# Sparse experts with routing counts read ahead of the norm, list transfers issued earlier, and attention's row of maxima sent by ScalarE

## The chip, the cores and the metric

The kernel runs on one core of one Trainium2 chip. The metric is the device time of one execution in microseconds (us). The engines are TensorE (PE, its weight loads PEld), VectorE (DVE), ScalarE (ACT), GpSimd (POOL) and SyncE (SP, which here only issues DMAs). Each engine works through its own list in order; semaphores tie them together.

## The reference

Six blocks on x of shape (16, 512, 256), each with a residual and a layer norm ahead of it: FFN, gated linear attention (GLA), FFN, experts, softmax attention, experts. The change touches the last three. Cut to what matters:

```python
def experts(x):                       # run twice: ahead of attention and behind it
    logits = x @ router_w + router_b                  # 8 experts, 8192 tokens
    topk_vals, topk_idx = top_k(logits, 2)
    gates = softmax(only the two chosen logits)
    routed = sum over the 2 chosen e: gates[e] * (silu(x @ w1[e]) * (x @ w3[e])) @ w2[e]
    shared = sum over 2 shared s:     (silu(x @ w1[s]) * (x @ w3[s])) @ w2[s]
    return routed + shared

def attention(x):                     # 16 sequences, 16 heads of 16
    scores = q @ k.T / 4 + band       # band: 0.1 where |i - j| <= 2
    return softmax(scores) @ v @ Wo.T + bo
```

All is float32; the kernel splits each matmul operand in a high and a low part (three matmuls for one product).

## The kernel before, in words

**Stages.** The blocks run one after another, with a barrier between them. x stays in SBUF. A batch is 512 tokens (4 tiles of 128); there are 16.

**Expert stage (`moe_stage`), first half, per batch b.** TensorE's list is: `hidden(b, 0)`, which is 12 matmuls of 512 columns for shared expert 0 (6 into h1, 6 into h3) with the 16 small router matmuls woven in; `output(b-1, 0)`; `transposes(b+1)`; `hidden(b, 1)`; `output(b-1, 1)`; `counts(b)`, which counts the tokens that each expert got. VectorE's list is: `product(b-1, 1)`; `normalise(b+1)` (L1152); `rows(b-1)` (L1190 to L1197), which reads the counts, adds them to `run` and works out the row of each token in its expert's list; `add_shared(b-2, 1)` (L1210); `product(b, 0)` (L1204); `choose(b)` (L1164 to L1185), which ranks the logits; `add_shared(b-1, 0)`; `low(b+1)` (L1159). ScalarE does silu (L1012), the high part of the activations (`act_high`, L1018), the high part of the transposed norm (L1007) and the two gates (L1023, L1024), with a table load at each change between silu and sigmoid. GpSimd does the low parts of the activations (`act_low`, L1108, one for each shared expert) and issues, for each batch, eight indirect DMAs (`enlist`, L1116) that write the normed rows to the experts' lists in HBM. Its order is `act_low(b, 0)`, `enlist(b-1)`, `act_low(b, 1)`.

Three waits order this: `hidden(b, 0)` starts with a wait for `counts_read` of batch b-1, which L1192 sets (the router writes the PSUM bank of the counts); `normalise(b)` waits until the lists of batch b-3 are written, since the buffer `m_rows` has three turns; and `output(b, 0)` waits for both low parts.

**Expert stage, second half.** When all counts are known, VectorE works out tables (L1243 to L1266), then 68 pairs of slots are loaded from the lists, put through their expert and scattered to `results`; then each token's two results are loaded and added.

**Attention (`att_stage`), per sequence.** 16 steps (4 groups of heads x 4 tiles) of two turns each. In each turn TensorE issues a pair of `s2` score matmuls for step st (L1642, which ScalarE turns to exponentials, L1804) and a pair of `s1` matmuls for step st+7 (L1628, from which VectorE takes the negated row maximum, L1898). The maxima of a group are transposed (L1653), copied by ScalarE (`max_copy`, L1814) and sent by a DMA into the row of `q_stack` that makes s2 come out with the maximum taken off (`max_row`, L1479, two DMAs from SP). Between them lie the transposes of the group's output (`out_t`, L1678, which also waits for `max_copy` of the group two further on) and the projections of the next sequence. q and k of the next sequence are written to HBM by SP (L1458) and read back in stacked form (L1471). SP's list for a sequence:

```python
def body(b, before, more):
    max_row(b, 1)
    write(b + 1, 0, x, False) for both x
    max_row(b, 2)
    write(b + 1, 0, x, True) for both x
    load(b + 1, 0); load(b + 1, 1)
    max_row(b, 3)
    ...
```

Of the kernel before, what the change touches and what calls it, by code (L numbers as in the profile page):

```python
# [77 lines left out]
def as_f32(ap):  # L78
    return ap.bitcast(F32)
# [579 lines left out]
ID_COL, ROW_COL = DM, DM + 1  # L659


def moe_stage(core, a, name, out=None):

# [8 lines left out]
    ROOM = ALL_TILES * P + P  # L672
    N_SLOTS = TOP_K * ALL_TILES + EXPERTS
    PAIRS = N_SLOTS // 2
# [3 lines left out]
    with ExitStack() as ctx:  # L678
# [11 lines left out]

        lists = nc.dram_tensor(name + "_lists", (EXPERTS * (ROOM + P), PITCH), F32).ap()
        results = nc.dram_tensor(name + "_results", (DUMMY + 2 * EXPERTS * TOP_K * P, DM), F32).ap()
# [22 lines left out]
        run_i = core.sbuf("run_i", [P, EXPERTS], I32, ctx)  # L715
        zeros = core.sbuf("zeros", [P, DM], F32, ctx)
        pad = core.sbuf("pad", [P, 2 * EXPERTS, PITCH - DM], F32, ctx)
        steps_of = core.sbuf("steps_of", [P, ALL_TILES], F32, ctx)
# [3 lines left out]
        over = core.sbuf("over", [P, EXPERTS, ALL_TILES], BF16, ctx)  # L722
# [7 lines left out]
        slot_lane_row = core.sbuf("slot_lane_row", [P, N_SLOTS], F32, ctx)  # L730
        slot_e_i = core.sbuf("slot_e_i", [P, N_SLOTS], I32, ctx)
        slot_row_i = core.sbuf("slot_row_i", [P, N_SLOTS], I32, ctx)
# [33 lines left out]
        high_ready, low_ready, y_ready, y_free = (s(f"{name}_{n}") for n in ("high", "low", "y", "y_free"))  # L766
# [25 lines left out]

        def results_of_pair(i):
            return results_written[i % YS_RING], 32 * (i // YS_RING + 1)

        with nc.Block() as block:

            @block.sync
            def _(sp):
# [4 lines left out]
                for e in range(EXPERTS):  # L804
                    rest = slice(EXPERTS * ROOM + e * P, EXPERTS * ROOM + (e + 1) * P)
                    sp.dma_start(lists[rest, 0:DM], zeros[:, :]).then_inc(padded, 16)
                    sp.dma_start(lists[rest, DM:PITCH], pad[:, EXPERTS + e, :]).then_inc(padded, 16)
                sp.wait_ge(run_ready, 1)
                for e in range(EXPERTS):
                    first = sp.value_load(run_i[0:1, e:e + 1], min_val=0, max_val=EXPERTS * ROOM - P)  # L810
                    sp.dma_start(lists[bass.ds(first, P), 0:DM], zeros[:, :]).then_inc(padded, 16)
                    sp.dma_start(lists[bass.ds(first, P), DM:PITCH], pad[:, e, :]).then_inc(padded, 16)
                sp.wait_ge(slots_ready, 1)
                sp.wait_ge(padded, 16 * 4 * EXPERTS)
                for r in range(XS_RING):
                    sp.wait_ge(listed[r], 16 * TILES * TOP_K * len(range(r, B, XS_RING)))
                for i in range(PAIRS):
                    if i >= XT_RING:
                        sp.wait_ge(t2_ready, i - XT_RING + 1)
                        sp.wait_ge(ids_ready, i - XT_RING + 1)  # L820
                    for j in range(2):
                        n = 2 * i + j
                        first = sp.value_load(slot_row_i[0:1, n:n + 1], min_val=0, max_val=EXPERTS * (ROOM + P) - P)
# [3 lines left out]
                by_lane = results[0:DUMMY, :].rearrange("(p n c) d -> p n c d", p=P, c=TOP_K)  # L827
                for i in range(PAIRS - YS_RING, PAIRS):
                    sp.wait_ge(*results_of_pair(i))
                if out is not None:  # L830
                    rows = out.rearrange("(n p) d -> p n d", p=P)
                for u in range(UNITS):
# [5 lines left out]
                    if out is not None and u >= YB_RING and (u - YB_RING) % 2 == 1:  # L838
                        tiles = slice((u - YB_RING - 1) * 2, (u - YB_RING + 1) * 2)
                        sp.dma_start(rows[:, tiles, :], core.x[:, tiles, :]).then_inc(stored, 16)  # L840
                if out is not None:
# [6 lines left out]
            def _(pe):  # L848
# [23 lines left out]
                def hidden(b, e):  # L872
# [3 lines left out]
                    if b:  # L876
                        pe.wait_ge(act_ready, 2 * (b - 1) + e + 1)
                        if e == 0:
                            pe.wait_ge(counts_read, b)
                    n = 0  # L880
                    for i, acc in enumerate((h1, h3)):
                        for k in range(KT):
                            for m, (w, x) in enumerate([(w13h, xh[p]), (w13l, xh[p]), (w13h, xl[p])]):
# [4 lines left out]
                                if e == 0:  # L888
                                    for _ in range(1 if n < 8 else 2):
# [89 lines left out]
                pe.wait_ge(slots_ready, 1)  # L979
# [20 lines left out]
            def _(act):  # L1000
# [42 lines left out]
                act.wait_ge(low_ready, 2 * B)  # L1043
# [24 lines left out]
            def _(pool):  # L1068
# [25 lines left out]
                link(g.iota(steps_of[:, :], pattern=[[P, ALL_TILES]], base=0, channel_multiplier=0,  # L1094
# [7 lines left out]
                link(g.iota(pad[:, :, 0], pattern=[[TOP_K * P, 2 * EXPERTS]], base=DUMMY, channel_multiplier=TOP_K,  # L1102
                            allow_small_or_imprecise_dtypes=True))

                def act_low(b, e):
                    pool.wait_ge(high_ready, 2 * b + e + 1)
                    slot = 2 * (b % 2) + e
                    nc.gpsimd.tensor_tensor(al[:, slot, :], act_f[:, e, :], as_f32(ah[:, slot, :]),  # L1108
                                            ALU.subtract).then_inc(low_ready, 1)
# [1542 lines left out]
```

## Time and profile before

| | |
|---|---|
| time before, median of 3 runs | 4055.28 us (4054.49 to 4057.51) |
| the profiled execution's own time | 4069.08 us |
| its span, first to last instruction | 4067.3 us |
| mean granted TensorE clock | 0.863 of full |
| busy shares of the span | PE 76%, DVE 61%, ACT 42%, POOL 38% |

Times inside the profile are counted from the span's start. Idle time stands just before the instruction that ended it, with what released it behind the arrow.

### The profile page before, as it was taken

To read this page: it belongs to the slowest core of one execution; us is meant where nothing else is said; L and a number is where in the kernel's file an instruction comes from. 1 tells how busy PE (TensorE), PEld (TensorE's weight loads), DVE (VectorE), ACT (ScalarE), POOL (GpSimd) and SP (SyncE) were. 2 spreads that over 40 slices of the span, in tenths; PEclk is the share of its full clock that TensorE was granted. 3 is DMA by queue.
4 is the path that set the end of the run, shared out by engine and by line. 5 is a ranking of instruction groups with operands and counts; after the bars stand their busy time and mean duration, and the time that the engine had idled before them with its cause. 6 is when DMAs were issued, how large, how long until landed. Compare 5 with 4: busy or idle time off the path is not lost. (4 is left out here: it accounts for less than half of the span.)

```text
span 4067.3 us, 73679 instructions
## 1 busy us (share of the span) xinstructions
PE 3094.8 (76%) x24796; PEld 2326.5 (57%) x24796; DVE 2478.4 (61%) x5047; ACT 1704.1 (42%) x2711; POOL 1564.5 (38%) x1380
## 2 busy tenths in 40 slices
PE   6998788886999566679417888888888875667892
PEld 4887677775888455579412333343333334556791
DVE  5665677776676444455656767666666644444566
ACT  2444344443455222246204555555555543222461
POOL 2555222221566344456312333333333322444561
PEclk9999899998999666689757999999999986666896
DMA  3000000000000111146533233332332302111568
GB/s 105 0 0 10 6 0 0 0 0 1 1 0 0 60 42 42 42 129 189 183 116 84 77 94 79 91 88 74 89 93 69 94 25 71 42 43 43 160 192 285
DMA packets 163468, 276.45 MB, mean 68 GB/s; under 512 B 28752, under 2 KB 100832, under 8 KB 163312
## 3 DMA queue, kind: packets, MB, share of 16 engines
q1 hardware_dynamic: 137968, 204.71, 18.2%
q0 software_dynamic: 25344, 69.76, 5.0%
q8 instruction: 85, 1.39, 0.2%
q14 instruction: 71, 0.58, 0.0%
HBM read 141.15 MB, written 132.71 MB: 67 GB/s over the span
## 5 line engine op out<-in xcount | busy, mean ns | idle before, releaser
L1898 DVE TENSOR_REDUCE neg_max_sb<-s_ps 128x2 f32<-128x1024 f32 x512 | 627.6, 1226 | 383.3 <-PE s_ps L1628 377.8
L1804 ACT ACTIVATE prob_sb<-s_ps 128x1024 f32<-128x1024 f32 x512 | 524.8, 1025 | 507.5 <-PE s_ps L1642 502.2
L1539 POOL TENSOR_TENSOR prob_sb<-prob_sb,band_sb 128x520 f32<-128x520 f32 (+1 forms) x256 | 284.9, 1113 | 728.6 <-ACT prob_sb L1804 728.6
L533 POOL TENSOR_TENSOR f_sq_lo_sb<-f_sq_sb,f_sq_hi_sb 128x512 fp32r<-128x512 f32 x256 | 329.2, 1294 | 349.7 <-ACT f_sq_hi_sb L508 349.6
L884 PE MATMUL moe_h_ps<-xnT_hi_sb,w13h_sb 128*128 128x512 f32 x256 | 150.9, 590 | 238.4 <-DVE run_sb L1192 234.4
L1628 PE MATMUL s_ps<-k_stack_sb,q_stack_sb 48*128 48x512 f32 x1024 | 249.0, 482 | 107.4 <-DMA k_stack_sb<-qk_scratch 53.6
L1130 POOL DMA_INDIRECT moe_results<-m_rows_sb,result_id_sb x272 | 260.8, 959 | 154.4 <-DVE result_id_sb L1281 100.5
L1665 PE MATMUL pv_ps<-prob_sb,v_ones_sb 128*32 128x512 f32 x2048 | 292.9, 646 | 1.4 <-POOL prob_sb L1539 1.3
L1642 PE MATMUL s_ps<-q_stack_sb,k_stack_sb 64*128 64x512 f32 x1024 | 267.0, 518 | 33.4 <-ACT prob_sb L1804 33.0
L1642 PEld LDWEIGHTS s_ps<-q_stack_sb,k_stack_sb 64*128 64x128 f32 x1024 | 99.4, 191 | 328.0 <-ACT prob_sb L1804 201.6
L503 ACT ACTIVATE f_relu_sb<-ffn_hp_ps 128x512 f32<-128x512 f32 x256 | 153.4, 599 | 314.7 <-PE ffn_hp_ps L456 314.1
L1116 POOL DMA_INDIRECT moe_lists<-m_rows_sb,row_i_sb x256 | 248.6, 971 | 73.3 <-issue 73.3
L570 DVE TENSOR_TENSOR f_sq_sb<-ffn_hp_ps,f_relu_sb 128x512 f32<-128x512 f32 x256 | 174.8, 687 | 134.3 <-ACT f_relu_sb L503 99.5
L468 PE MATMUL ffn_y_ps<-w_proj_tern_sb,f_sq_lo_sb 128*128 128x256 f32 x1024 | 256.1, 283 | 0.0
L468 PE MATMUL ffn_y_ps<-w_proj_tern_sb,f_sq_hi_sb 128*128 128x256 f32 x1024 | 255.1, 282 | 0.7 <-POOL f_sq_lo_sb L533 0.7
L1108 POOL TENSOR_TENSOR m_act_lo_sb<-m_act_sb,m_act_hi_sb 128x512 fp32r<-128x512 f32 x64 | 90.1, 1408 | 400.9 <-ACT m_act_hi_sb L1018 400.2
L456 PE MATMUL ffn_hp_ps<-xnT_hi_sb,w_fc_hi_sb 128*128 128x512 f32 x512 | 210.7, 412 | 20.6 <-DVE xnT_lo_sb L162 19.8
L1012 ACT ACTIVATE m_silu_sb<-moe_h_ps 128x512 f32<-128x512 f32 x64 | 38.2, 597 | 447.7 <-PE moe_h_ps L884 447.4
L1204 DVE TENSOR_TENSOR m_act_sb<-moe_h_ps,m_silu_sb 128x512 f32<-128x512 f32 x64 | 44.3, 692 | 282.0 <-ACT m_silu_sb L1012 264.7
L884 PEld LDWEIGHTS moe_h_ps<-xnT_hi_sb,w13h_sb 128*128 128x128 f32 x256 | 65.1, 254 | 251.4 <-issue 236.3
L1628 PEld LDWEIGHTS s_ps<-k_stack_sb,q_stack_sb 48*128 48x128 f32 x1024 | 104.1, 200 | 182.6 <-DVE neg_max_sb L1898 120.1
L456 PE MATMUL ffn_hp_ps<-xnT_hi_sb,w_fc_lo_sb 128*128 128x512 f32 x512 | 203.9, 398 | 0.0
(353 smaller groups left out, 8964.7 us busy)
## 6 DMA issues: line engine op xcount, KB each, us to landing
m_rows_sb<-moe_lists SPq DMA_DIRECT2D x272, 130.0 KB
qk_scratch<-qk_hi_sb SPq DMA_DIRECT2D x128, 256.0 KB
q_stack_sb<-qk_scratch SPq DMA_DIRECT2D x128, 192.0 KB, 3.6
k_stack_sb<-qk_scratch SPq DMA_DIRECT2D x128, 192.0 KB, 4.6
xnT_hi_sb<-moe_results SPq DMA_DIRECT2D x32, 512.0 KB, 3.8
xnT_lo_sb<-moe_results SPq DMA_DIRECT2D x32, 512.0 KB, 5.1
qk_scratch<-qk_lo_sb SPq DMA_DIRECT2D x64, 256.0 KB
x_resident_sb<-x SPq DMA_DIRECT2D x4, 2048.0 KB, 17.8
```

The lines of the kernel that those rows point to most:

```text
L456: op = nc.tensor.matmul(hp[j % 2][:, :], a[:, k, j * P:(j + 1) * P], x[:, k, :], start=(k == 0 and i == 0), stop=(k == KT - 1 and i == 2))
L468: op = nc.tensor.matmul(y[:, t, :], r[:, j, t * P:(t + 1) * P], w.proj[:, j, :], start=(j == 0 and t % 2 == 0 and i == 0), stop=(j == JT - ...
L533: nc.gpsimd.tensor_tensor(sql[:, j, :], sq[:, j % 2, :], as_f32(sqh[:, j, :]), ALU.subtract).then_inc(low_ready, 1)
L884: op = nc.tensor.matmul(acc[e][:, :], w[:, EXPERTS + e, k, i, :], x[:, k, :], start=(k == 0 and m == 0), stop=(k == KT - 1 and m == 2))
L1116: g.indirect_dma_start(lists, bass.IndirectOffsetOnAxis(row_i[:, r, t, c:c + 1], 0), xs[:, r, t, :], None).then_inc(listed[r], 16)
L1130: g.indirect_dma_start(results, bass.IndirectOffsetOnAxis(result_id[:, i % ID_RING, j:j + 1], 0), rows_out[:, i % YS_RING, j, :], None).th ...
L1539: nc.gpsimd.tensor_tensor(pr, pr, bcast(band[:, off:off + hi - lo].unsqueeze(1), [P, GH, hi - lo]), ALU.mult).then_inc(band_done, 1)
L1628: op = nc.tensor.matmul(s1p[:, half, :], qs[r, g // 2, at, qt * P:(qt + 1) * P], ks[r, g // 2, at, :], start=True, stop=True)
L1642: op = nc.tensor.matmul(s2p[:, half, :], ks[r, g // 2, at, kt * P:(kt + 1) * P], qs[r, g // 2, at, :], start=True, stop=True)
L1665: op = nc.tensor.matmul(pvp[2 * HD * i:2 * HD * (i + 1), :], vaug[:, kt, GH * g + i, :], prob[:, kt, i, :], start=(kt == 0), stop=(kt == T ...
L1804: nc.scalar.activation(prob[:, kt, pair(t), :], s2p[:, :, :], ACT.Exp).then_inc(exp_done, 1)
L1898: nc.vector.tensor_reduce(nm[:, g % 2, pair(t), qt], s1p[:, :, :], AXIS_X, ALU.max, negate=True).then_inc(max_done, 1)
```

## The change

What it does, with one "wave" (`WAVES = 1`), so that the new loops over waves run once:

- VectorE: `rows(b-1)` stands ahead of `normalise(b+1)`; behind it a new `act_low(b-1)` makes the low part of shared expert 1.
- GpSimd: one low part for each batch (expert 0), and `enlist(b-1)` ahead of it. The semaphore of the low parts is split in two.
- TensorE: `hidden(b, 0)` waits for the counts to be read behind the 7th matmul, not ahead of the 1st, and all 16 router matmuls stand among the last 6.
- Tables: one small copy more (`run` is reset), and two casts become adds.
- Second half: the order of waits on SP is a little different; the work is the same.
- Attention: `max_copy` moves up one turn; `max_row` goes from SP to ScalarE, two turns' places: behind the exponentials of (st % 4 == 2, first turn).

```diff
# TensorE, hidden(b, e)
                     if b:
                         pe.wait_ge(act_ready, 2 * (b - 1) + e + 1)
-                        if e == 0:
-                            pe.wait_ge(counts_read, b)
...
-                                if e == 0:
-                                    for _ in range(1 if n < 8 else 2):
+                                if e == 0 and i == 1:
+                                    if b and n == 0:
+                                        pe.wait_ge(counts_read, b)
+                                    for _ in range(2 if n < 4 else 3):
                                         router(b, n)
# TensorE, output(b, half)
-                        pe.wait_ge(low_ready, 2 * b + 2)
+                        for e in range(SHARED):
+                            pe.wait_ge(low_ready[e], b + 1)
# GpSimd
                 for b in range(B):
-                    act_low(b, 0)
                     if b:
                         enlist(b - 1)
-                    act_low(b, 1)
+                    act_low(b)
                 enlist(B - 1)
# VectorE
+                def act_low(b):
+                    dve.wait_ge(high_ready, 2 * b + 2)
+                    slot = 2 * (b % 2) + 1
+                    v.tensor_tensor(al[:, slot, :], act_f[:, 1, :], as_f32(ah[:, slot, :]),
+                                    ALU.subtract).then_inc(low_ready[1], 1)
...
                     if b:
                         product(b - 1, 1)
+                        rows(b - 1)
+                        act_low(b - 1)
                     if b + 1 < B:
                         normalise(b + 1)
-                    if b:
-                        rows(b - 1)
                     if b >= 2:
                         add_shared(b - 2, 1)
                     product(b, 0)
# tables
+                    link2(v.tensor_copy(run[:, :], first_row[:, :]))
# attention, SP
                 def body(b, before, more):
-                    max_row(b, 1)
...
+                    for m in range(KT):
+                        if more:
+                            for low in (False, True):
+                                for x in range(2):
+                                    write(b + 1, m, x, low)
+                            load(b + 1, 2 * m)
+                            load(b + 1, 2 * m + 1)
# attention, ScalarE
+                def max_row(b, g):
+                    act.wait_ge(nmt_ready, b * GROUPS + g + 1)
+                    hold(act, row_turns)
+                    places = slice(place(g, 0), place(g, 0) + 2)
+                    for half in range(2):
+                        row, of = 64 * half + STACK, slice(half * 2 * TILES, (half + 1) * 2 * TILES)
+                        act.dma_start(as_f32(qs[row:row + 1, g // 2, places, :]),
+                                      as_f32(nmt[of, g % 2, :])).then_inc(rowed[g], 16)
...
-                            if st % TILES == 2 and t == 0:
-                                if st - 1 + TILES < STEPS:
-                                    max_copy(b, st // TILES + 1)
+                            if st % TILES == 1 and t == 1 or st % TILES == 2 and t == 0:
+                                step = max_copy if t else max_row
+                                if st // TILES + 1 < GROUPS:
+                                    step(b, st // TILES + 1)
                                 elif more:
-                                    max_copy(b + 1, 0)
+                                    step(b + 1, 0)
```

## Rows read from the trace of the kernel before

**Rows 1.** Windows by stage: busy us (count) of PE, PEld, DVE, ACT, POOL; clock, DMA.
```profile
1365.00:1760.00 395.00, 265.55 (x1208) 234.53 (x1208) 167.59 (x496) 103.26 (x161) 160.23 (x165) 0.67 0.12 43
2160.00:3300.00 1140.00, 963.14 (x5530) 437.89 (x5532) 773.95 (x931) 625.57 (x779) 382.38 (x320) 0.93 0.33 83
3375.00:3770.00 395.00, 264.41 (x1208) 232.77 (x1208) 167.06 (x495) 103.26 (x161) 159.55 (x163) 0.68 0.12 43
```

**Rows 2.** The waits of 1395 to 1757: us in total, times, longest.
```profile
PE moe_h_ps L884 <- DVE run_sb L1192: 110.4, 14, 8.8
DVE m_rows_sb L1152 <- DMA moe_lists<-m_rows_sb,row_i_sb: 73.1, 13, 6.3
```

**Rows 3.** The timeline of one batch, VectorE and GpSimd: start, duration.
```profile
1581.48 0.69 DVE L1204 TENSOR_TENSOR m_act_sb<-moe_h_ps,m_silu_sb 128x512 f32<-128x512 f32 x1 [7.93 <-ACT m_silu_sb L1012]
1582.09 0.18 DVE L1164 TENSOR_TENSOR logits_sb<-moe_misc_ps,router_b_sb 128x32 f32<-128x32 f32 x1
...
1586.60 0.75 DVE L1210 SCALAR_TENSOR_TENSOR x_resident_sb<-moe_y_ps,x_resident_sb 128x256 f32<-128x256 f32 x2
...
1595.92 1.38 DVE L1152 TENSOR_SCALAR m_rows_sb<-x_resident_sb,ln_mean_var_sb,ln_rstd_sb 128x256 f32<-128x256 f32 x4 [6.06 <-DMA moe_lists<-m_rows_sb,row_i_sb]
...
1582.90 1.52 POOL L1108 TENSOR_TENSOR m_act_lo_sb<-m_act_sb,m_act_hi_sb 128x512 fp32r<-128x512 f32 x1 [12.68 <-ACT m_act_hi_sb L1018]
...
1593.46 0.96 POOL L1116 DMA_INDIRECT moe_lists<-m_rows_sb,row_i_sb  x1 [0.30 <-issue]
```

**Rows 4.** Windows inside two batches, columns as in rows 1.
```profile
1572.30:1583.10 10.80, 10.73 (x38) 9.60 (x39) 2.73 (x11) 1.22 (x2) 0.20 (x1) 0.50 0.00 0
1583.10:1589.00 5.90, 5.77 (x38) 4.86 (x37) 5.20 (x13) 4.41 (x7) 4.83 (x5) 0.98 0.19 67
1589.00:1597.50 8.50, 0.22 (x6) 0.12 (x5) 2.24 (x7) 0.75 (x2) 5.47 (x6) 0.77 0.22 79
```

**Rows 5.** The timeline of the stage's last batch, which has no `normalise`.
```profile
1743.22 0.17 DVE L1192 TENSOR_TENSOR run_sb<-moe_misc_ps,run_sb 128x8 f32<-128x8 f32 x1
1743.54 0.47 PE L884 MATMUL moe_h_ps<-xnT_hi_sb,w13h_sb 128*128 128x512 f32 x1 [1.43 <-DVE run_sb L1192]
1748.12 0.60 ACT L1012 ACTIVATE m_silu_sb<-moe_h_ps 128x512 f32<-128x512 f32 x1 [4.38 <-PE moe_h_ps L884]
1757.08 0.17 DVE L1192 TENSOR_TENSOR run_sb<-moe_misc_ps,run_sb 128x8 f32<-128x8 f32 x1
1763.48 1.85 POOL L1116 DMA_INDIRECT moe_lists<-m_rows_sb,row_i_sb  x1 [0.16 <-issue]
```

**Rows 6.** Two lines: duration ns min/median/max, first and last start.
```profile
L1192 DVE TENSOR_TENSOR run_sb<-moe_misc_ps,run_sb x32: 166/166/168, 1393.4 to 3767.7; 128x8 f32<-128x8 f32 x32
L1479 SPq DMA_DIRECT2D q_stack_sb<-neg_max_t_sb x128: 634/674/1061, 2146.3 to 3314.5; - x128
```

**Rows 7.** Windows in GLA and in attention, columns as in rows 1.
```profile
455.00:970.00 515.00, 424.61 (x8600) 370.90 (x8598) 402.42 (x845) 214.51 (x351) 121.39 (x101) 1.00 0.00 0
2863.70:2870.00 6.30, 6.25 (x21) 2.90 (x21) 2.45 (x2) 1.60 (x2) 0.73 (x1) 0.50 0.30 64
```

**Rows 8.** The waits of 2202 to 3240, attention's inner sequences.
```profile
PE misc_ps L1678 <- ACT neg_max_t_sb L1814: 58.4, 56, 1.1
PE s_ps L1628 <- DMA k_stack_sb<-qk_scratch: 40.2, 14, 3.3
```

**Rows 9.** One of the page's costliest groups: busy us, mean ns, idle before.
```profile
L1804 ACT ACTIVATE prob_sb<-s_ps 128x1024 f32<-128x1024 f32 x512 | 524.8, 1025 | 507.5 <-PE s_ps L1642 502.2
```

**Rows 10.** The timeline of SP's issues between two sequences.
```profile
2850.14 1.76 SPq L1479 DMA_DIRECT2D q_stack_sb<-neg_max_t_sb  x2
2852.04 1.33 SPq L1458 DMA_DIRECT2D qk_scratch<-qk_lo_sb  x2
```

**Rows 11.** The timeline of ScalarE in the batch of rows 3.
```profile
1585.63 1.28 ACT L1023 ACT_TABLE_LOAD   x1
1586.92 0.21 ACT L1023 ACTIVATE gates_sb<-lead_sb 128x4 f32<-128x4 f32 x1
```

More of the change, by code:

```diff
@@ L765, in moe_stage @@
         h_ready, silu_ready, act_ready = (s(f"{name}_{n}") for n in ("h", "silu", "act"))
-        high_ready, low_ready, y_ready, y_free = (s(f"{name}_{n}") for n in ("high", "low", "y", "y_free"))
+        high_ready, y_ready, y_free = (s(f"{name}_{n}") for n in ("high", "y", "y_free"))
+        low_ready = [s(f"{name}_low{e}") for e in range(SHARED)]
         logits_ready, chosen_ready, counts_ready, counts_read = (
@@ L803, in _, with load_rows @@
                 sp.wait_ge(consts, CONSTS)
[L804 to L814, printed above, removed]
+                for w in range(WAVES):
+                    for e in range(EXPERTS):
+                        row = w * WAVE_ROWS + EXPERTS * ROOM + e * P
+                        sp.dma_start(lists[row:row + P, 0:DM], zeros[:, :]).then_inc(padded, 16)
+                        sp.dma_start(lists[row:row + P, DM:PITCH],
+                                     pad[:, (2 * w + 1) * EXPERTS + e, :]).then_inc(padded, 16)
+                for w in range(WAVES):
+                    sp.wait_ge(run_ready, w + 1)
+                    for e in range(EXPERTS):
+                        first = sp.value_load(run_i[0:1, w, e:e + 1], min_val=0, max_val=WAVES * WAVE_ROWS - P)
+                        sp.dma_start(lists[bass.ds(first, P), 0:DM], zeros[:, :]).then_inc(padded, 16)
+                        sp.dma_start(lists[bass.ds(first, P), DM:PITCH],
+                                     pad[:, 2 * w * EXPERTS + e, :]).then_inc(padded, 16)
+                sp.wait_ge(padded, 16 * 4 * EXPERTS * WAVES)
                 for r in range(XS_RING):
                     sp.wait_ge(listed[r], 16 * TILES * TOP_K * len(range(r, B, XS_RING)))
-                for i in range(PAIRS):
+                by_lane = results[0:DUMMY, :].rearrange("(p n c) d -> p n c d", p=P, c=TOP_K)
+                if out is not None:
+                    rows = out.rearrange("(n p) d -> p n d", p=P)
+                def load_rows(i):
                     if i >= XT_RING:
@@ L822, in _, with load_results @@
                         n = 2 * i + j
-                        first = sp.value_load(slot_row_i[0:1, n:n + 1], min_val=0, max_val=EXPERTS * (ROOM + P) - P)
+                        first = sp.value_load(slot_row_i[0:1, n:n + 1], min_val=0, max_val=WAVES * WAVE_ROWS - P)
                         sp.dma_start(rows_in[:, i % XT_RING, j, :], lists[bass.ds(first, P), :]).then_inc(
                             rows_in_loaded[i % XT_RING], 16)
[L827 to L832, printed above, removed]
+                def load_results(u):
+                    w = u // WAVE_UNITS
+                    if u % WAVE_UNITS == 0:
+                        for i in range((w + 1) * WAVE_PAIRS - YS_RING, (w + 1) * WAVE_PAIRS):
+                            sp.wait_ge(*results_of_pair(i))
                     if u >= YB_RING:
@@ L837, in _ @@
                         results_loaded[u % YB_RING], 16)
-                    if out is not None and u >= YB_RING and (u - YB_RING) % 2 == 1:
+                    if out is not None and u >= YB_RING and u % 2:
                         tiles = slice((u - YB_RING - 1) * 2, (u - YB_RING + 1) * 2)
                         sp.dma_start(rows[:, tiles, :], core.x[:, tiles, :]).then_inc(stored, 16)
+                sp.wait_ge(slots_ready, WAVES)
+                for i in range(PAIRS):
+                    load_rows(i)
+                    if unit_at(i + 1) is not None:
+                        load_results(unit_at(i + 1))
+                for u in range(UNITS - WAVE_UNITS, UNITS):
+                    load_results(u)
                 if out is not None:
@@ L1472, in load @@
                                          scratch[m, x, :, :, heads, :]).then_inc(loaded[g], 16)
-                def max_row(b, g):
-                    sp.wait_ge(nmt_ready, b * GROUPS + g + 1)
-                    places = slice(place(g, 0), place(g, 0) + 2)
-                    for half in range(2):
-                        row, of = 64 * half + STACK, slice(half * 2 * TILES, (half + 1) * 2 * TILES)
-                        sp.dma_start(as_f32(qs[row:row + 1, g // 2, places, :]),
-                                     as_f32(nmt[of, g % 2, :])).then_inc(rowed[g], 16)
                 for m in range(KT):
```

180 lines of the change are left out of this document (93 added, 87 removed).

## The prediction, made before the changed kernel was run

> **What bounds the kernel now.** I read the page first (no engine is busy throughout), then the windows by stage, then the waits inside the stages that the diff touches, then one batch in order of time.
>
> The windows show where time is lost [rows 1]: each expert stage's first half takes about 395 us with TensorE busy 265 of them, and that at a granted clock of 0.67, so much of the busy time is slow matmuls. Attention has 963 busy of 1140 us at 0.93. The waits name the loss [rows 2]: in one first half TensorE stands 110 us before `hidden(b, 0)` until L1192 has read the counts, and VectorE stands 73 us before `normalise` until the lists of three batches back are written. One batch in order of time shows that these are one chain [rows 3]. `act_low(b, 0)` starts at 1582.90, only then come the eight list DMAs, 0.30 and 0.96 us each, the last at 1593.46; it lands about 1.5 us after its 0.96, `normalise` runs at 1595.92, `rows` behind it, and only then `hidden(b+1, 0)`. So a batch lasts as long as hidden + silu + product + low part + eight DMAs + landing + norm. The clock makes it worse [rows 4]: after the idle 8.5 us the next 10.8 us run at 0.50, until TensorE has been busy a while.
>
> The interval is (1743.2 - 1393.4)/14 = 25.0 us for 14 batches [rows 5, 6]. The last batch has no `normalise` and so no list wait ahead of `rows`; it took 1757.08 - 1743.22 = 13.9 us [rows 5]. This is the nearest thing in the trace to the changed order.
>
> **The change in the first half.** With `rows` first and `enlist(b-1)` ahead of `act_low(b)`, list DMAs start as soon as the rows are known, a whole interval before `normalise` asks for them. I add up what each engine must do for a batch at full clock:
>
> - VectorE: product 0.61, choose 4.51 (1582.09 to 1586.60), add 0.7, low 1.3 (two of the product's size), product 0.6, rows 1.0 (six small ones like L1192's 0.17), norm 1.4, add 0.7 come to 10.8, and the new `act_low`, two operands of 128x512 like the product, is 0.69: 11.5 [rows 3, 5].
> - GpSimd: 8 x 1.26 + one low part of 1.5 = 11.7 (before: 13.2) [rows 3].
> - TensorE: half of 10.7 slow plus 5.8 fast is 11.1 [rows 4]. Of it `hidden(b, 0)` is 4.58 from first matmul to silu [rows 5]; the rest I share out by columns as an estimate: `hidden(b, 1)` 2.7, two outputs at 1.4, transposes 1.0, counts 0.4. With latencies 11.4.
>
> All three lie close together, so the interval is a loop through them. The longest that I find starts at silu(b, 0): silu and product 0.63 + 0.61, choose 4.51, `add_shared` 0.75 (which frees y), `output(b-1, 1)` 1.4, counts 0.4, `hidden(b+1, 0)` 4.58 to its silu. That is 12.9, with five crossings of some 0.05 us 13.2. The counts no longer lie on it: L1192 is done about 9.3 us after silu(b, 0), and the 7th matmul ends about 10. The list wait does not either: eight DMAs from the rows on take 10.3, landing 1.5, so 11.8 us against an interval of 13.2 plus the 0.7 of `act_low`. The spare is only 2 us. TensorE then has one gap of about 1.9 us per batch (y not yet free).
>
> The clock decides the rest. Between two levels: at full clock 13.2. If the lower one held all the time TensorE would be busy throughout at 22.8. The evidence is divided. In GLA 515 us passed at 1.00 with TensorE busy 82% [rows 7], and here it would be 11.4/13.2 = 86%. In attention, behind a stall of 2.9 us, 6.3 us ran at 0.50 [rows 7]. The gap here is 1.9 us, shorter than that stall but once in each batch. TensorE's part of the loop is 6.4 us, so a mean clock of 0.9 gives 13.9. I take 14.0.
>
> Per stage: 363.7 us from the first L1192 to the last before [rows 5, 6], 15 x 14.0 = 210 after: 154 saved. The last batch's lists start at 1763.5 before, because two low parts and the batch before's lists stand in front [rows 5]; after, they start with the rows at about 1758: 5 more. The stage enters at the lower clock and stays there a batch or so: 5 back. The extra copy in the tables is 0.2. So 154 a stage, **308** for two; the second stage's windows repeat the first's [rows 1]. In the second half nothing is on another engine than before: 0.
>
> **Attention.** Two waits of TensorE change [rows 8]. `out_t` waits for `max_copy`, 58.4 us in 56 places, 1.04 each: the copy stood behind an exponential of 1.03 us [rows 9]. It moves ahead of it, so the wait goes. At three of the four places of a sequence the step has work to fill in; at the step with the other stall, it is swallowed. Second, `s1` waits for the stacked k, 2.9 us in each of 14 sequences. On SP the low writes stood behind `max_row`: 2850.14 against 2852.04 [rows 10]. Taking the row away brings writes, loads and landing forward by 1.9 us. Together 3 x 0.9 + 1.9 = 4.6 us per sequence; a part will turn into other waits, since the step's two turns also hang on VectorE's maxima, so I take 3.8, x 15 = **57**.
>
> What ScalarE pays: two issues per group. SP needs 0.67 us for one [rows 6]; no row shows a DMA issued by ScalarE. If its sequencer issues while the exponential runs (1.03 us), 1.35 us is hidden in that and in the gap of over 1 us before the next one; if it waits for it, each group loses 1.35 on the exp loop, 5.4 a sequence, which takes all the 4.6 and a little more. Above: 4.6 and, without the slow 6.3 us behind the stall [rows 7], up to 3 more. So attention gains from -15 to 115, and I take 57, nearer to hidden. The Trainium skill says ("DMA: Bandwidth & Descriptors", section "Issuing engines are not separate DMA queues") that spreading issues over engines saves only the issuing sequencer's time. By that rule alone, attention would gain at most SP's 1.76 us per sequence [rows 10], 26 us, and not 57; the rule leaves out that the order of SP's list, and `max_copy`'s place on ScalarE, change too.
>
> One more rule speaks against my interval. ScalarE loads two tables per batch, which delays silu(b, 1). The row says 1.28 and the next ACTIVATE 0.01 us behind it [rows 11]. The skill ("ScalarE: Activation LUTs", section "What ACT_TABLE_LOAD costs") adds a drain of about 1.38 us to each switch; estimated by that page, silu(b, 1), the product and the rows would come 2.8 us later and the interval would be about 15.7. The trace does not have this drain, and it decides; what a late silu would do is inside rival 1's interval.
>
> **Sum.** 308 + 57 = 365. Against the profiled execution's own 4069.1 that is 3704; the median of the runs lies 13.8 lower, so **3690** there (-9.0%).
>
> **The rivals.**
>
> 1. *The clock doesn't hold.* The gap of 1.9 us and the stretch of small router matmuls just ahead of it bring the lower level in every batch. For it: before, ten slow us passed with TensorE 99% busy in just such work before the clock rose [rows 4]. Against: GLA. With a mean of 0.7 TensorE's 6.4 us are 9.1 and the interval about 16.3: 119 a stage with the ends left at 0, total 4055 - 238 - 40 = 3777. The skill ("TensorE: Matmul & The Clock Gate", section "HAM oscillation — how this bites in real kernels") also tells of kernels that fall back in each turn of a loop; in rows 4 this one does. Held at 0.5 throughout, 22.8: 3975.
> 2. *ScalarE's issues stand in the exp loop*, above: attention gains nothing or loses 15, total 4055 - 308 + 8 = 3755.
> 3. *GpSimd or the lists become the bound.* The lists of one batch are written twice as often. A list DMA took 1.85 us in one place, beside a bf16 table instruction of VectorE [rows 5]. At 1.85 each the interval is 8 x 1.85 + 1.5 = 16.3: like rival 1, 3775. **Slower than before** it gets only when GpSimd's `enlist` needs over 3.1 us for each DMA: the mean interval before, 363.7/15 = 24.2, and 57/30 = 1.9 for attention's gain make 26.1, less 1.5 for the low part, over 8. At 3.5 us the interval is 29.5 and the total 4055 + 30 x 5.3 - 57 = 4157. Nothing in the rows goes that far.
> 4. *The change does nothing*: the wait for the lists only moves, since `normalise` still stands on VectorE ahead of `product(b, 0)`. It would need landing some 10 us later than now. 4055 within 0.2%.
>
> **Chances.** My forecast (interval 13.2 to 14.8, attention 20 to 110; 3625 to 3735) 0.58; rival 1 0.17, of which the lower level throughout 0.03; rival 2 0.14; rival 3 0.06, of which slower 0.02; rival 4 0.02; the remaining 0.03 is for more than I foresee (clock at 1.00 in attention too). Range: 3620 to 3800 takes in the forecast, rival 2 and most of rivals 1 and 3. Under 0.2% (8 us) a measurement of this kernel can't tell from no change. Faster 0.96, same 0.015, slower 0.025.
>
> **What would show it.** The interval of L1192 (or its line after) from 25.0 to 13 to 15 us; the clock of the first halves from 0.67 to 0.9 or more; no wait of TensorE for `run` over 1 us, and one of about 1.9 before `output(b-1, 1)` for the residual add; VectorE's wait before `normalise` under 1 us; each first half at 235 to 250 us. In attention: no wait of `out_t` for the row of maxima, the wait for the stacked k at 1 to 1.5 us, exponentials no later behind ScalarE's issues. The prediction is wrong if the clock falls in each batch, if the list DMAs stretch, or if L1804 is held up at every fourth step.

## The result, and the profile after

The changed kernel takes 3667.5 us (median of 4 runs, 3658.1 to 3674.2) against 4056.4 us for the kernel before on the same chip: a ratio of 0.904, interval 0.902 to 0.906. The forecast was 3690 in a range of 3620 to 3800. The profiled execution is the fastest of the four, 3658.1 us with a span of 3656.3 and so 9.4 below the median, where that of before was 12.7 above its own (4069.1 against 4056.4). So 22 of the 411 us between the two spans lie in which executions were profiled, and 389 in the kernels.

The windows of the changed kernel by stage (us of the window, busy us and count of PE, PEld, DVE, ACT and POOL, granted clock, DMA share, GB/s). They stand against [rows 1]:

```profile
1390.00:1584.00 194.00, 181.26 (x1147) 161.67 (x1145) 155.16 (x481) 95.79 (x150) 139.15 (x136) 0.94 0.23 83
1960.00:3070.00 1110.00, 971.56 (x5510) 444.35 (x5510) 780.26 (x937) 623.20 (x775) 379.76 (x318) 0.92 0.34 87
3165.00:3365.00 200.00, 183.94 (x1177) 163.47 (x1176) 163.78 (x502) 100.27 (x157) 142.66 (x138) 0.95 0.23 82
```

In the first half TensorE is now busy 93% of the time, not 67%, and its clock is 0.94, not 0.67. The busy time fell too. From the first count of the stage to the last, so over the same matmuls, it went from 250 to 180 us: most of them are no longer run at half speed. Here is the line that reads the counts, L1224 (L1192 before), against the first row of [rows 6]:

```profile
L1224 DVE TENSOR_TENSOR run_sb<-moe_misc_ps,run_sb x32: 166/166/169, 1391.4 to 3359.8; 128x8 f32<-128x8 f32 x32
```

Within a stage it comes 15 intervals apart from 1391.4 to 1581.2 and from 3173.2 to 3359.8: 12.65 and 12.44 us on average, where the first 14 were 25.0.

The batches are not alike. Here are three of these intervals in a row (columns as above):

```profile
1481.50:1493.10 11.60, 11.38 (x78) 10.01 (x77) 9.98 (x33) 6.36 (x11) 8.27 (x9) 1.00 0.23 81
1493.10:1505.40 12.30, 11.58 (x79) 10.40 (x78) 10.57 (x33) 6.37 (x11) 9.24 (x10) 1.00 0.24 88
1505.40:1519.10 13.70, 12.80 (x79) 11.66 (x78) 10.59 (x33) 6.42 (x11) 10.19 (x10) 0.88 0.25 90
```

In the third the clock was 0.50 for 3.4 us. Over both stages, 11 of the 30 intervals hold a stretch at 0.50 and last 13.7 us on average; the other 19 hold none and last 11.9. So the mean clock of 0.94 is 1.00 with such stretches in it.

The waits in the first stage's batches, 1391 to 1583 us, against [rows 2]:

```profile
DVE m_act_sb L1237 <- ACT m_silu_sb L1044: 31.4, 23, 2.7
...
PE moe_y_ps L944 <- DVE x_resident_sb L1249: 9.2, 15, 1.1
...
DVE m_rows_sb L1184 <- DMA moe_lists<-m_rows_sb,row_i_sb: 0.9, 1, 0.9
...
PE moe_misc_ps L898 <- DVE run_sb L1224: 0.2, 1, 0.2
```

The 110 us of TensorE for the counts and the 73 us of VectorE for the lists are gone. What is left to TensorE is a wait for the residual add, at most 1.1 us in each batch.

By place, the span lost 2.0 us ahead of the first L1224 (L1192), 173.9 in the first stage's batches, 54.3 from there to the second stage's first batch, 177.6 in the second stage's batches and 3.1 behind them. Of the 54.3, attention's 15 sequences hold 41.3 (from the first second-pass matmul to that of the last sequence, 1112.2 us before and 1070.9 after). The waits of attention's inner sequences, 2050 to 2990 us, show that the one for the row of maxima, 58 us in [rows 8], has no row any more. The one for the stacked k, 3.2 us in each of 13 sequences, has not shrunk (2.9 before):

```profile
PE s_ps L1659 <- DMA k_stack_sb<-qk_scratch: 41.7, 13, 3.7
PE s_ps L1673 <- ACT prob_sb L1835: 31.4, 53, 0.9
PE s_ps L1659 <- DVE neg_max_sb L1940: 24.5, 29, 1.3
```

### The profile page after: what moved, and what is told of

Read it like the earlier page. It is cut to its first block and busy times, and to the rows that moved or that the text cites. A ratio compares the mean times of both kernels' runs of the same rounds, so it can differ in the third digit from the quotient of the medians.

```text
span 3656.3 us, 73695 instructions
## 1 busy us (share of the span) xinstructions
PE 2955.9 (81%) x24796; PEld 2208.2 (60%) x24796; DVE 2474.6 (68%) x5081; ACT 1704.4 (47%) x2711; POOL 1521.9 (42%) x1348
## 5 line engine op out<-in xcount | busy, mean ns | idle before, releaser
L456 PE MATMUL ffn_hp_ps<-xnT_lo_sb,w_fc_hi_sb 128*128 128x512 f32 x512 | 201.6, 394 | 0.0
L468 PEld LDWEIGHTS ffn_y_ps<-w_proj_tern_sb,f_sq_hi_sb 128*128 128x128 f32 x1024 | 194.4, 190 | 11.9 <-POOL f_sq_lo_sb L533 1.1
L468 PEld LDWEIGHTS ffn_y_ps<-w_proj_tern_sb,f_sq_lo_sb 128*128 128x128 f32 x1024 | 195.2, 191 | 10.0
L2458 POOL TENSOR_TENSOR g_ks_sb<-g_ks_sb,g_tot_sb 128x512 f32<-128x512 f32 x96 | 109.1, 1137 | 178.0 <-PE g_h_ps L2206 117.6
L200 DVE BATCH_NORM_STATS2 ln_stat_sb<-x_resident_sb 128x6 f32 (+1 forms) x384 | 138.2, 412 | 35.6 <-POOL x_resident_sb L541 21.7
```

The source lines that it names most:

```text
L456: op = nc.tensor.matmul(hp[j % 2][:, :], a[:, k, j * P:(j + 1) * P], x[:, k, :], start=(k == 0 and i == 0), stop=(k == KT - 1 and i == 2))
L468: op = nc.tensor.matmul(y[:, t, :], r[:, j, t * P:(t + 1) * P], w.proj[:, j, :], start=(j == 0 and t % 2 == 0 and i == 0), stop=(j == JT - ...
```

## The experiments

**The two parts alone.** `m_only` takes all expert edits and leaves attention as before, `a_only` the reverse.

> The expert stages changed, attention as before. If the two parts do not touch each other (theory A), the interval between batches in the first halves is 12.6 us as in the changed kernel's trace, each first half 174 to 178 us shorter, and attention's sequences last 75 us as before: about 3712 us. My prediction's sizes (308 us for the experts) would give 3748 us. If attention's change had also helped the experts (clock, queues), it would be above 3760.

> Attention changed, the expert stages as before. Theory A: sequences of 71.6 us as in the changed kernel's trace, 41 us less, about 4015 us. My prediction's size (57 us) would give 3999 us. TensorE's wait for the stacked k stays near 3 us in each sequence if the writes' transfer bounds it, and falls to 1 to 1.5 us if SP's order does.

`m_only` took 3702.7 us (ratio 0.9125, interval 0.9105 to 0.9144) and `a_only` 4022.1 (0.9915, 0.9892 to 0.9938), with 4061.4 for the kernel before in these runs. So the experts give 359 us and attention 39, both near theory A. They add up to 398, against 389 measured with both; each of the three has an interval of 8 us or more to either side, so the 9 us between them are not clear of noise. The intervals between batches in `m_only` are those of the full change (12.4 on average), and no run shows the two parts touching each other.

**The two halves of attention's edit.** `copy_early` is the kernel before with `max_copy` one turn earlier, and SP still sends the row. `row_act` leaves the copy at its old place, and ScalarE sends the row behind it. The edit of `copy_early`:

```diff
-                            if st % TILES == 2 and t == 0:
+                            if st % TILES == 1 and t == 1:
                                 if st - 1 + TILES < STEPS:
                                     max_copy(b, st // TILES + 1)
```

> The kernel before with one edit: ScalarE copies the row of maxima one turn earlier; SP still sends it, in the old order. Theory B (the copy's place is the whole of attention's gain): as a_only, some 41 us, 4015 us. Rival (my prediction: 2.7 us of a sequence from the copy, 1.9 from SP's freed order): about 33 us less than before, 4023 us, and a_only 15 to 25 us below it.

> The kernel before with the other edit alone: ScalarE sends the row, behind the copy at its old place, and SP's list is free of it. Theory B: SP's low writes start some 2 us earlier, but land no earlier, the wait for the stacked k stays at 2.9 us, and the time stays within 5 us of before (4051 to 4061 us). Rival (my prediction): 1.9 us of each sequence, 28 us less, 4028 us. If ScalarE's issues stand in the way of the exponentials: slower by up to 5.4 us a sequence, 4135 us.

`copy_early` took 4025.0 us (0.9912, 0.9881 to 0.9943), the gain of `a_only` but for 3 us. In the two profiled executions the 15 sequences are 7 us longer in `copy_early` (1078.4 against 1071.4), so the row's move may have a small part of its own beside the copy; neither number is clear of noise. `row_act` took 4074.7 (1.0033, 1.0021 to 1.0046), 13 us slower than before, where theory B had said no change. Its waits of 2202 to 3240 us, against [rows 8]:

```profile
PE misc_ps L1658 <- ACT neg_max_t_sb L1794: 58.3, 56, 1.1
...
PE s_ps L1608 <- DMA k_stack_sb<-qk_scratch: 23.1, 13, 2.4
...
PEld s_ps L1622 <- DMA q_stack_sb<-neg_max_t_sb: 18.4, 13, 1.7
```

The wait for the row of maxima stays. The one for the stacked k falls by some 17 us and comes back as a wait for the row itself, which ScalarE now sends late. Timed from the end of the keys' cast (`high_part` of x = 1), which is what makes the writes possible, the mean over 14 sequences is:

| from the end of the cast, us | before | row_act | after |
|---|---|---|---|
| first low write issued | 3.55 | 1.42 | 1.42 |
| first load issued | 9.18 | 9.09 | 8.90 |
| group 0 of the stack landed | 15.15 | 15.10 | 14.87 |

SP's list without the row issues the low writes 2.1 us earlier, and the loads start when they did. What they wait for is not SP.

**The order on GpSimd.** `low_first` is the changed kernel with `act_low(b)` ahead of `enlist(b-1)` again.

```diff
 for b in range(B):
+    act_low(b)
     if b:
         enlist(b - 1)
-    act_low(b)
```

> The changed kernel with GpSimd's low part of batch b put back ahead of the list DMAs of batch b-1. Theory C (this order closed the chain of before): list DMAs of b-1 start only behind hidden, silu, product, cast and low part of b, the norm two batches on waits for their landing, and the next low part hangs on that: 10.3 + 1.5 + norm 1.4 + add 0.7 + product 0.65 + cast 1.35 + low part 1.4 = some 17.5 us, more at a lower clock: 17.5 to 19 us for a batch, 150 to 190 us more than the changed kernel, 3815 to 3860 us. Rival D (VectorE's order, rows ahead of the norm, did it): within 30 us of the changed kernel, 3670 to 3700 us.

It took 3771.0 us (0.9287, 0.9267 to 0.9307): 104 of the 389 us gained are lost, more than D said and less than C. The mean interval of the first stage is 16.1. The waits of its batches, 1394 to 1629 us:

```profile
POOL m_act_lo_sb L1141 <- ACT m_act_hi_sb L1050: 77.2, 15, 10.5
...
PE moe_y_ps L944 <- DVE x_resident_sb L1249: 45.9, 15, 4.7
...
DVE m_rows_sb L1184 <- DMA moe_lists<-m_rows_sb,row_i_sb: 41.7, 13, 4.9
```

GpSimd stands in front of its low part with the lists ready behind it, and the wait for the lists is back. Two more things are in the 3.6 us that a batch got longer: one multiply of `choose` costs 1.0 more (last section), and 28 of the 30 intervals hold a stretch at the clock of 0.50, where 11 did. That it stops at 16 and not at 25 fits `rows` no longer waiting behind `normalise`; no run has both orders put back.

**The order on VectorE.** `norm_first` is the changed kernel with `rows(b-1)` and the new `act_low` behind `normalise(b+1)`.

```diff
         product(b - 1, 1)
-        rows(b - 1)
-        act_low(b - 1)
     if b + 1 < B:
         normalise(b + 1)
+    if b:
+        rows(b - 1)
+        act_low(b - 1)
```

> The changed kernel with VectorE's rows put back behind the norm. Theory C: the lists start 1.4 us later and so the loop lists 10.3 + landing 1.5 + norm 1.4 = 13.3 us decides: 0.6 us more for a batch, 20 us more in all, 3690 us. Rival D: counts are read late again, most of the gain of the experts is gone, over 3850 us.

3732.8 us (0.919, 0.917 to 0.921), interval 14.6 and 14.8 in the two stages: 65 us lost, where C said 20 and D over 180. Waits of 1394 to 1612 us:

```profile
PE moe_misc_ps L898 <- DVE run_sb L1224: 21.6, 14, 2.5
DVE m_rows_sb L1184 <- DMA moe_lists<-m_rows_sb,row_i_sb: 9.4, 8, 1.9
```

The wait of TensorE for the counts, which is D's, is back at 1.5 us in each of 14 batches; C's wait for the lists comes in 8 and is shorter. Each batch lasts 2.1 us longer, and 19 of the 30 intervals hold a stretch at 0.50. So the result lies between the two theories, nearer to C by its size and to D by its waits. With the lists started early, `normalise` ahead of `rows` costs 65 us; with `rows` ahead, a late start of the lists costs 104. Either order, kept with the other edits, holds most of the gain.

**The place of the wait on TensorE.** `wait_head` makes the counts wait ahead of all of `hidden(b, 0)`, as before, and spreads the router's matmuls over it.

```diff
         pe.wait_ge(act_ready, 2 * (b - 1) + e + 1)
+        if e == 0:
+            pe.wait_ge(counts_read, b)
```

> The changed kernel with TensorE's wait for the counts back at the head of the first hidden matmuls and the router spread over all of them. By my prediction's walk the counts are read 9.3 us behind the silu and the matmuls could start at 8.4: 0.9 us of each batch where it lies on the loop: 15 to 27 us more, 3685 to 3695 us. Rival: TensorE has other waits to fill, nothing to see (within 8 us of 3667).

3685.7 us (0.9073, 0.9056 to 0.909), 18 us for it, as expected (14 by the ratios). But the trace puts the cost elsewhere: the first intervals of the two stages are 17.6 and 16.6 us, at the low clock, against 11.2 and 12.3, and make 11 us. Behind them TensorE waits 0.9 us for the counts in each batch, the clock stays at 1.00, and every interval is 12.9, against 12.6 on average in the changed kernel with its stretches at 0.50.

**The low part on VectorE.** `pool_both` puts the second low part back on GpSimd.

```diff
 def act_low(b):
-    pool.wait_ge(high_ready, 2 * b + 1)
+    for e in range(SHARED):
+        pool.wait_ge(high_ready, 2 * b + e + 1)
```

> The changed kernel with both low parts on GpSimd. GpSimd then needs 8 x 1.26 + 2 x 1.35 and its own waits, 13.3 us for a batch, and the low parts lie beside more of VectorE's two-operand work. Theory E (GpSimd becomes the bound, and VectorE's operations with both operands in SBUF stretch beside its subtraction as the multiply of choose did before, 1.38 against 0.42): 13.3 to 14.3 us, 20 to 50 us more, 3690 to 3720 us, and the stretched operations show in the trace. Rival F (VectorE was the long pole with 11.5 us and is relieved of 0.69): 10 to 20 us less, 3650 us.

3695.1 us (0.9093, 0.9067 to 0.9119), 28 us more, and steady intervals of 13.7 in the second stage (13.5 on average in the first, from 11.2 to 16.2): theory E. GpSimd then waits only some 0.9 us of such an interval, for the cast; eight DMAs with their issues and two low parts fill the rest. Each of these intervals also holds 3.4 us at the clock of 0.50, and how much of the 13.7 is that was not separated.

**The sigmoids off the path.** `gates_late` is the changed kernel with one pair of sigmoids at the end of the first half, over all batches, in the place of a pair in each batch. Its result stands in the table below, with those of the next two.

```diff
-                    share(b)
                     silu_of(b, 1)
                     act_high(b, 1)
+                share()
```

> The changed kernel, with the two sigmoids of each batch put off to the end of the first half (one pair of sigmoids over all batches; nothing is left out). In the changed kernel two table loads of 1.28 us each and the sigmoids stand on ScalarE ahead of the second silu of each batch, and VectorE waits 31 us a stage for silu. Theory G, what is left between batches is partly this wait: the interval falls from 12.5 to 11.8 or 12.0, where TensorE's own 11.7 us of work per batch stops it; 2 stages x 15 x 0.6 = 18 us, so 3640 to 3655 us. Rival H, TensorE's work alone sets the interval and VectorE's wait is idle time that costs nothing: 3663 to 3672 us, interval 12.4 to 12.7.

**The keys' cast one exponential earlier.** `high_early` is the changed kernel with this edit of ScalarE's order in attention; `late_and_early` has both edits.

```diff
+                            if more and at in ((4, 0), (5, 0)):
+                                high_part(b + 1, 0, st - 4)
                             if st % TILES == 1 and t == 0:
                                 if st > 1:
                                     ot_copy(b, st // TILES - 1)
...
-                            if more and at in ((4, 0), (5, 1)):
-                                high_part(b + 1, 0, t)
```

> The changed kernel, with the cast of the keys' high part for the next sequence made one exponential earlier (behind the first exponential of the sixth step, ahead of the copy of the output; nothing is left out). The stacked keys are waited for 3.1 us in each sequence. Theory T, the chain of transfers from that cast to the loaded stack (14.9 us, whatever SP's order) sets the wait: the cast ends 2.0 us earlier, the stacked keys land 1.5 to 2.0 us earlier, the wait falls to 1.1 to 1.6 us, and 15 x 1.5 to 2.0 makes 22 to 30 us: 3637 to 3645 us. Rival S, the transfers are set by something other than that cast (the queue's other loads, the rows of maxima): wait 2.8 to 3.1 us and 3663 to 3672 us. Rival X, the cast ahead of the output's copy delays the exponentials by 0.6 us a sequence or more: above 3672 us or the gain less than half.

> Both edits of the two runs beside this one in one kernel. If both theories hold they add: 3667 less 18 less 26 is 3623 us, range 3610 to 3640. If either fails, the other's time alone.

| kernel | median us | ratio to before | interval |
|---|---|---|---|
| changed kernel | 3667.5 | 0.9039 | 0.9017 to 0.906 |
| gates_late | 3649.6 | 0.8993 | 0.897 to 0.9016 |
| high_early | 3612.8 | 0.891 | 0.8883 to 0.8937 |
| late_and_early | 3605.2 | 0.8885 | 0.8864 to 0.8907 |

`gates_late`: the mean intervals fell from 12.65 and 12.44 to 12.37 and 12.24, 7 us in all. The spans differ by 5 and the medians by 18. It is nearer to H by the traces: the intervals without a stretch at 0.50 went from 11.88 to 11.78 on average, 0.1 us and not 0.6, and the long ones, 13.0 to 16.1, are those with such a stretch, 7 where 11 had one. It is a small gain whose size these runs don't settle.

`high_early` gave 55 us (45 by the spans of the profiled executions), about twice what theory T said. T was right in its place. The stack lands 14.98 us behind the cast, as in the changed kernel (14.87), the cast ends 1.9 us earlier, and TensorE's wait fell from 3.1 to 1.2 us per sequence. But the mean sequence got 3.0 us shorter, 71.4 to 68.4, and only 1.9 of that is the wait. The windows show the rest. First the changed kernel, ending its wait at 2665.6 (columns as above):

```profile
2662.60:2665.00 2.40, 0.00 (x0) 0.00 (x0) 0.22 (x1) 1.27 (x2) 0.31 (x1) 1.00 1.03 201
2665.60:2667.60 2.00, 2.00 (x7) 1.43 (x8) 1.23 (x1) 0.00 (x0) 0.00 (x0) 0.72 1.07 203
2667.60:2669.60 2.00, 2.00 (x7) 0.76 (x5) 0.00 (x0) 0.26 (x1) 0.00 (x0) 0.50 0.18 37
2669.60:2671.60 2.00, 2.00 (x15) 0.55 (x13) 1.23 (x1) 1.57 (x4) 1.11 (x1) 0.92 0.00 0
```

And the same steps of the same sequence in `high_early`, its wait ending at 2633.9:

```profile
2630.90:2633.30 2.40, 1.62 (x12) 0.34 (x10) 1.88 (x2) 1.75 (x2) 1.12 (x1) 1.00 1.00 215
2633.90:2635.90 2.00, 1.97 (x8) 1.24 (x8) 1.23 (x1) 0.17 (x1) 0.00 (x0) 1.00 1.01 209
2635.90:2637.90 2.00, 2.00 (x16) 0.65 (x15) 1.20 (x1) 1.44 (x3) 0.34 (x1) 1.00 0.03 6
2637.90:2639.90 2.00, 2.00 (x16) 1.57 (x18) 1.26 (x2) 1.35 (x3) 0.79 (x1) 1.00 0.01 2
```

Behind the wait of 3.3 us TensorE's clock falls to 0.50 (1.2 GHz) for 3.4 us, and in a window of 2 us at that clock seven matmuls pass where sixteen do at 2.4 GHz. Over the 15 sequences the two add up: the waits for the stack fell from 46.3 to 17.6 us, 28.7 less, and the time at 0.50 from 152.5 to 121.1 us, which at half speed is 15.7 us of TensorE's work. Together they make 44.4, and the sequences got 44.6 us shorter.

But a long wait doesn't always bring the low clock, nor a short one spare it. In the changed kernel such a stretch lies at 14 of the 15 waits (1.7 to 3.7 us), not at one of 2.84. In `row_act` it lies at the 11 waits of 1.59 to 2.43 us and at none of the four of 0.15 to 1.09. In `high_early` it lies at two of 14, 1.51 and 1.83, and not at 1.62 or 2.05. `late_and_early` has the best time of all, 3605.2 us, though no more than 8 us below `high_early`; it lies 5 us under the range expected, since `high_early` alone gave more than was put in.

## Why the prediction was right, and where its numbers were off

**The loop through the list DMAs was the bound: right.** Both waits went, the clock of the first halves rose to 0.94 and 0.95, and `low_first` and `norm_first` bring the waits back one at a time. So rival 4 fell too. Each wait comes back in part, and no run puts back both orders. The first halves' batches gave 351.5 us by the spans, where the prediction took 308 with their ends. Of these ends it took 5 us saved at the tail and 5 given back at the entry. Neither came. The lists of the first stage end 4.2 us sooner behind the last count, but the first load from them starts 19.6 us behind it, where it was 19.4; and the first batches of a stage (11.2 and 12.3 us) are no longer than the mean. The 13.0 us that the spans show between the stages beside attention's 15 sequences (54.3 - 41.3) lie in its last sequence (4.5) and between attention and the next stage's first count (8.2). `m_only`, with attention as before, has 4.5 and 7.2 in the same places; what makes them is open.

**The interval, forecast 14.0, is 12.55.** One batch checks the forecast's loop term by term. It ran at the clock of 1.00, for which the forecast said 13.2, and TensorE waits in it for the residual add (0.72 us), so the loop has no slack there. The changed kernel's ScalarE, VectorE and GpSimd in order of time:

```profile
1496.57 0.60 ACT L1044 ACTIVATE m_silu_sb<-moe_h_ps 128x512 f32<-128x512 f32 x1 [2.86 <-PE moe_h_ps L913]
...
1508.67 0.60 ACT L1044 ACTIVATE m_silu_sb<-moe_h_ps 128x512 f32<-128x512 f32 x1 [2.66 <-PE moe_h_ps L913]
...
1497.85 0.17 DVE L1196 TENSOR_TENSOR logits_sb<-moe_misc_ps,router_b_sb 128x32 f32<-128x32 f32 x1
...
1499.08 0.43 DVE L1203 TENSOR_TENSOR notless_sb<-notless_sb,earlier_sb 128x256 f32<-128x256 f32 x1
...
1501.40 0.75 DVE L1249 SCALAR_TENSOR_TENSOR x_resident_sb<-moe_y_ps,x_resident_sb 128x256 f32<-128x256 f32 x2
...
1505.57 0.88 DVE L1225 TENSOR_TENSOR placed_sb<-at_place_sb,row_at_sb 128x64 f32<-128x64 f32 x1
...
1505.06 1.30 POOL L1141 TENSOR_TENSOR m_act_lo_sb<-m_act_sb,m_act_hi_sb 128x512 fp32r<-128x512 f32 x1
```

Silu to silu is 12.10 us: silu and product 1.28 (forecast 1.24), `choose` 3.55 (4.51), the add 0.75 (0.75), and from there through the output, the counts and `hidden` to the next silu 6.52 (6.38, and 0.25 of crossings). The step that was mis-sized is `choose`. The 4.51 was read from the trace of before, and in it L1171 (L1203 now) took 1.38 us and not 0.43, because it stood beside GpSimd's low part. The change moved that low part away, and the price of a VectorE instruction changed with it. Part of the price moved on: the low part now often stands beside L1225 of `rows`, which takes 0.21 us alone in 12 batches and 0.31 to 1.56 in the other 20 (0.88 in the rows above).

The clock's term was nearly right: 0.8 us was added for it (13.2 to 14.0), and the 11 long intervals of 30 make 0.7 (12.55 against 11.9).

**The clock holds in most batches (rival 1 fell, but not far).** Rival 1 had the lower level come in every batch; it comes in 11 of 30, for 3.4 us each but for one of 6.8 and one of 1.9, and each costs about 1.8 us. The gap ahead of `output(b-1, 1)` is at most 1.1 us and not 1.9, since `choose` is shorter. What brings the low stretches is open: `wait_head`, with a gap of 0.9 us in every batch, has none past its first ones. Rival 3 fell as well. The list DMAs stay at 0.96 us in the median (39 of 256 took 1.1 to 1.5), but it is not far away: with one more low part GpSimd is busy nearly throughout (`pool_both`, 13.7). The drain of 1.38 us at each change of table, which the Trainium skill states ("ScalarE: Activation LUTs", "What ACT_TABLE_LOAD costs") is not in this trace either. ScalarE of the same batch:

```profile
1501.13 1.28 ACT L1055 ACT_TABLE_LOAD   x1
1502.42 0.21 ACT L1055 ACTIVATE gates_sb<-lead_sb 128x4 f32<-128x4 f32 x1
...
1502.74 1.28 ACT L1044 ACT_TABLE_LOAD   x1
1504.03 0.60 ACT L1044 ACTIVATE m_silu_sb<-moe_h_ps 128x512 f32<-128x512 f32 x1
```

**Attention, forecast 57, gave 39** (`a_only`; 41 by the spans). Of its two steps one failed: "Taking the row away brings writes, loads and landing forward by 1.9 us". The writes are issued 2.1 us earlier, and the landing comes 0.05 (`row_act`) to 0.3 us (changed kernel) earlier. SP's order was not the last thing that the loads waited for. What is left between the last write's issue (3.55 us behind the cast) and the first load (8.90) is the writes themselves, six of 256 KB, four of them issued behind the cast. Whether it is their transfer was not tried by making them smaller; that the chain hangs on the cast was tried (`high_early`) and held. The prediction stopped at the queue where it should have followed the data. The other step held: the place of `max_copy` alone gives 36 us (`copy_early`), 2.4 per sequence for the 2.7 foreseen.

**Rival 2 fell: ScalarE's issues are hidden.** The exponential and the issue run side by side:

```profile
2578.83 1.02 ACT L1835 ACTIVATE prob_sb<-s_ps 128x1024 f32<-128x1024 f32 x1 [0.32 <-PE s_ps L1673]
2578.91 1.42 ACTq L1853 DMA_DIRECT2D q_stack_sb<-neg_max_t_sb  x2
2580.45 1.02 ACT L1835 ACTIVATE prob_sb<-s_ps 128x1024 f32<-128x1024 f32 x1 [0.60 <-PE s_ps L1673]
```

The rule of the Trainium skill ("DMA: Bandwidth & Descriptors", "Issuing engines are not separate DMA queues"), set against the forecast as at most 26 us, came out right for its part: moving the issues gained nothing by itself (`row_act`, 1.0033), and all but at most a few us of the gain are in `max_copy`.

**The sum.** Experts 359 for 308 and attention 39 for 57 are two misses of opposite sign, 51 and 18, and the parts' sum is 9 above the whole, which is not clear of noise. That the forecast of 3690 is only 23 us off is partly luck: with the experts' miss alone it would have been 51.

## What to carry to other kernels

When a loop runs through two engines' orders, find which instruction stands in front of what the other needs; here putting either order back cost 65 or 104 us of the 389 gained, and the other edits kept the rest. A duration read from the trace holds only beside the same neighbours: if the change moves a GpSimd tensor instruction, price the VectorE instructions beside it again. And follow a late load back along its data, to the cast and the writes, before crediting the queue that issues it; a wait on TensorE can cost more than its length, when the clock falls behind it. Last, look at the single batches before taking a mean clock as a steady one: 0.94 was 1.00 with a stretch of 3.4 us at 0.50 in every third batch.

## What the runs showed of the hardware

**A VectorE instruction with its operands in SBUF that starts beside a GpSimd tensor_tensor waits for its end.** Before, L1171 overlapped GpSimd's low part in 32 of 32 batches and took 1374 to 1408 ns. After, L1203 stands away from it in 30 batches and takes 424 to 427 ns; in the first batch of each stage it still stands beside it and takes 1395 and 1399. `low_first` moves only the GpSimd instruction, and the time is back, 1382 to 1401 ns in 32 of 32. Its VectorE and GpSimd:

```profile
1510.38 1.38 DVE L1203 TENSOR_TENSOR notless_sb<-notless_sb,earlier_sb 128x256 f32<-128x256 f32 x1
...
1509.96 1.52 POOL L1141 TENSOR_TENSOR m_act_lo_sb<-m_act_sb,m_act_hi_sb 128x512 fp32r<-128x512 f32 x1 [4.96 <-ACT m_act_hi_sb L1050]
```

VectorE's multiply, asked for 0.42 us into GpSimd's, ends 0.28 us behind it. In `pool_both` it also takes one with a single operand in SBUF, of 8 columns, which is 0.16 us by itself and ends here 0.03 us behind GpSimd's:

```profile
3260.00 1.26 DVE L1230 TENSOR_SCALAR row_i_sb<-row_f_sb 128x8 uint32<-128x8 f32 x1
...
3259.93 1.30 POOL L1142 TENSOR_TENSOR m_act_lo_sb<-m_act_sb,m_act_hi_sb 128x512 fp32r<-128x512 f32 x1 [0.90 <-ACT m_act_hi_sb L1050]
```

The longest in that kernel was 3.20 us, beside two low parts. VectorE instructions with one operand in PSUM are not held: in the changed kernel L1237 took 692 ns in the median in the 25 places beside GpSimd's tensor_tensor and 691 in the 39 away from it, and L1224 166 and 167. One already under way is mostly not held either: L1170, the instruction ahead of L1171, starts 0.03 us before GpSimd's (0.10 in two batches) and takes 418 to 420 ns in all 32 batches of before. But L1225 was held once, in the changed kernel, for 1.56 us though it had started 0.19 us ahead; how far under way it must be is open.

**Two more.** A DMA issued by ScalarE takes 627 ns at the least and 638 in the median (2.04 us at the most), in the rows above beside a running ACTIVATE, much as SP's 634 and 674 [rows 6]. And TensorE's clock falls from 1.00 to 0.50 for 3.4 or 6.8 us at a time in otherwise busy stretches: at 14 of 15 waits of 1.7 to 3.7 us in attention (changed kernel), at 2 of 14 of 0.1 to 2.1 us (`high_early`), and in 11 of 30 expert batches whose longest gap is 1.1 us. The length of the gap alone doesn't tell which.
